# Norm guard and layernorm eps as pair reductions on VectorE, and the layer's input added one step sooner on GpSimd, in a two-block attention kernel

## Chip, cores and metric

The kernel runs on one core of a Trainium2 chip. The metric is the device time of one execution in microseconds; where several runs are given, their median stands with the lowest and the highest.

## The reference

The input is 16 sequences of 256 tokens with 128 channels, float32. Two blocks follow each other, each closed by a layernorm without gain over `x + block(x)`.

The first block is a gated depthwise convolution and a 16-head attention in which the keys are softmaxed in chunks of 64. The change does not touch it.

The second block has two layers. Cut to what matters, one of them is:

```python
h = shift_token(x); q, k, v = split(h @ wqkv)          # 8 heads of 64
q = q / clip(norm(q), 1e-12) * qs;  k = k / clip(norm(k), 1e-12) * ksc
q, k = rotary_xpos(q, k)
x = x + local_attention(q, k, v) @ wo                  # windows of 64, each sees itself and the one before
h = shift_token(x); h = (h - mean(h)) / sqrt(var(h) + 1e-5) * lg + lb
a, g = split(h @ w1 + b1)
x = x + (a * gelu(g)) @ w2 + b2
```

After the second layer the block's input is added once more and the last layernorm is taken.

## The kernel before, in words

Every engine has an instruction list of its own, written out by hand, with semaphores between them. Stage A computes the first block. Then the two layers run as one pipeline over 32 units, a unit being one sequence of one layer: 16 units of layer 0, then 16 of layer 1. A unit has two steps, one for each half of its tokens (`tile` 0, the even step, and `tile` 1, the odd step). In its steps each engine does work of several units, at lags that `F_LATE` sets in steps: the layernorm statistics of a unit come 4 steps after its scores, the GELU gates 6, the product of gates and values and the down projection 7, its residual sum `yo` 8, the final normalisation `zo` 9. A loop body holds four steps, that is two units.

In each step of the layers:

- TensorE computes the scores (L1427, L1434), transposes the normalised weights of the step before (L1448) as soon as GpSimd has normalised them (`f_normed`), makes the output projection (L1473), the projections of the next unit (L1360), the transposes of its q and k (L1365, after `qk_normed`), the weighted values (L1462) and pieces of the MLP (L1378, and the down projection L1399 at the end of the odd step, after VectorE's `uT`).
- VectorE takes the score maximum (`fmx`, L1191) and subtracts it (L1195). In odd steps the low part of the next input (L1141), the first product `uT` and the normalised middle `hc` (L1091) follow; in even steps `yo` (L1122), in layer 1 with the statistics of `yo`. Then `rotate` (L1072, L1073 and the reduction L1076 of the squares), `mid` (L1156), the sum of the exponentials (L1173) and its reciprocal (L1177). In odd steps the last two products `uT` (L1099) come next, in even steps the statistics of the middle (L1082, L1086). A second `rotate` ends the step, and in odd steps of layer 1 `zo` (L1134).
- GpSimd does for each of the two `rotate`s: the sum of the two rotated products (L649), the maximum of the squared norm with a floor (L657), the power -0.5 (L660) and the multiplication by it (L663). Between the two it normalises five of the eight heads' weights (L710) and, in even steps, takes the middle's rstd in two instructions, the eps addition (L684) and the power (L686). In layer 1 it adds the layer input at the end of an odd step (`residual`, L694), and begins odd steps with the rstd of `yo`, again L684 and L686.
- ScalarE squares the projections (L801), copies from PSUM, takes the exponentials (L893), scales three heads (L870) and computes the GELU (L848), each with a table load where the function changes. In layer 0 it keeps a copy of `mid` (`kept`, L863) where layer 1 has the residual; it reads the same entry of `F_LATE`.
- SyncE issues the DMAs in an order of its own: for each unit the loads of `hn` and `res`, the shifts of `mid` into `mn` (32 KB pieces), in layer 1 the load of `res1`, which the residual adds, and the stores.

What waits for what around the change:

- GpSimd's power waits for `guarded`, which today its own maximum sets; the maximum waits for `norm_step` of VectorE's reduction.
- VectorE's `mid` of a unit waits until the residual of the unit two before it is made (`resb_set` in layer 1, `mid_kept` in layer 0), since it writes the same buffer.
- The residual waits for both halves of `mid` of its unit, for `yo` of the unit two before it (`f_read["down"]`, the buffer `resb`) and for its DMA (`res1_in`).
- `hc` waits for `m_rstd`, `zo` for `z_rstd`.

Of the kernel before, what the change touches and what calls it, by code (L numbers as in the profile page):

```python
# [25 lines left out]
P = 128  # L26
# [12 lines left out]
PAIR = 2  # L39
# [8 lines left out]
F_LATE = {"stats": 4, "norm": 5, "residual": 5, "mT": 6, "gates": 6, "mix": 6, "values": 7, "down": 7, "yo": 8, "z": 9}  # L48
# [123 lines left out]
def build(nc, t):  # L172

    ctx = ExitStack()
    with ctx:
# [82 lines left out]
        norm2 = sb("norm2", [P, 2, 4 * F_HEADS])  # L258
# [29 lines left out]
        mmv = [sb(f"mmv{p}", [P, TILES, 2]) for p in range(PAIR)]  # L288
        mrstd = [sb(f"mrstd{p}", [P, 2, TILES]) for p in range(PAIR)]
        zstat = [sb(f"zstat{p}", [P, TILES, 6]) for p in range(PAIR)]  # L290
        zmv = [sb(f"zmv{p}", [P, TILES, 2]) for p in range(PAIR)]
# [45 lines left out]
        N_CONSTS, N_F_CONSTS, N_PADS = 7, 6, 4  # L337
# [254 lines left out]
        def _(pool):  # L592
            pool.memset(ones[:, :], 1.0).then_inc(consts_set, 1)
            pool.memset(halves[:, :], -0.5).then_inc(consts_set, 1)
            pool.memset(eps[:, :], LN_EPS).then_inc(consts_set, 1)
            for p in range(PAIR):
                pool.memset(uT[p][:, F_CHUNKS - 1, :], 1.0).then_inc(consts_set, 1)
# [46 lines left out]
            def layers_program():  # L644
# [7 lines left out]
                def normalise(unit, m):  # L652

                    at, index = slice(F_HEADS * m, F_HEADS * (m + 1)), 4 * unit + m
                    pool.wait_ge(consts_set, N_CONSTS)
                    pool.wait_ge(norm_step, index + 1)
                    nc.gpsimd.tensor_scalar_max(norm2[:, 1, at], norm2[:, 0, at], NORM_FLOOR).then_inc(guarded, 1)  # L657
                    pool.wait_ge(guarded, index + 1)
                    wait(pool, qk_normed, index - 3)
                    nc.gpsimd.tensor_tensor(out=rnorm[:, at], in0=norm2[:, 1, at], in1=halves[:, 0:F_HEADS], op=ALU.pow).then_inc(rnorm_set, 1)  # L660
# [20 lines left out]
                def rstd_of(mv2, out, step, done, stats, count):  # L681

                    pool.wait_ge(stats, TILES * (count + 1))
                    nc.gpsimd.tensor_tensor(out=out[:, 0, :], in0=mv2[:, :, 1], in1=eps[:, 0:TILES], op=ALU.add).then_inc(step, 1)  # L684
# [12 lines left out]
                def body(it, turn, layer_of):  # L697
                    for s, p, tile in f_steps(turn):
                        n, unit = F_STEPS * it + s, PAIR * it + p
                        local = f_late(turn, s, "z")  # L700
                        if local is not None and layer_of(local) == LAYERS - 1:
                            rstd_of(zmv[local % PAIR], zrstd[local % PAIR], z_eps, z_rstd, z_stats, PAIR * it + local - BATCH * (LAYERS - 1))
# [10 lines left out]
                        if local is not None:  # L713
                            rstd_of(mmv[local % PAIR], mrstd[local % PAIR], m_eps, m_rstd, m_stats, PAIR * it + local)
# [206 lines left out]
        def _(dve):  # L921
# [137 lines left out]
            def layers_program():  # L1059
                def rotate(index, before, local, m, turn, layer):  # L1060
# [15 lines left out]
                    nc.vector.tensor_reduce(norm2[:, 0, F_HEADS * m:F_HEADS * (m + 1)],  # L1076
                                            sq[m % 2][:, :].rearrange("p (h d) -> p h d", h=F_HEADS), AX.X, ALU.add).then_inc(norm_step, 1)

                def stats(x, st, out, bn, done, count):
# [5 lines left out]
                    for tile in range(TILES):  # L1085
                        nc.vector.bn_aggr(out[:, tile, :], st[:, tile, :]).then_inc(done, 1)  # L1086
# [490 lines left out]
```

## Time and profile before

| | us |
|---|---|
| median of 3 runs | 1403.01 (1402.93 to 1405.08) |
| the profiled execution | 1405.44 |
| its span | 1403.6 |
| VectorE busy | 1231.8 (88%) |
| GpSimd busy | 943.0 (67%) |
| TensorE matmul busy | 1249.5 (89%) |
| ScalarE busy | 944.8 (67%) |

The busy times come from the profiled execution, whose own time stands in the second line; what lies outside its span is 1.8 us. Shares are means over two stages with different limits: up to about 690 us the first block runs, after it the two layers. Instructions of one engine overlap at their ends in the records, so a next one may start some hundredths before the last one's end.

### The profile page before, as it was taken

Reading aid. Unit: us, or ns where it says so; the run is one execution under the profiler, and the core shown is the slowest. Engines: PE = TensorE matmul, PEld = TensorE weight load, DVE = VectorE, ACT = ScalarE, POOL = GpSimd, SP = SyncE. Lnnn points to the kernel's source line nnn. Section 1 sums busy time; section 2 is a strip of 40 time slices with the busy share of each in tenths; the row PEclk is TensorE's granted clock in tenths of the full one; section 3 lists DMA queues with packets and bytes.
Section 4 is the critical chain, followed back from the end, with each engine's and each line's share of the span. In section 5 each row is a group of like instructions: output and inputs, shape, how many; then the busy total and the mean of one; then the engine's idle time right before and its main releaser. Section 6 shows DMA issues by size and latency. Waiting matters only on the chain.

```text
span 1403.6 us, 36296 instructions
## 1 busy us (share of the span) xinstructions
PE 1249.5 (89%) x12288; PEld 977.4 (70%) x12288; DVE 1231.8 (88%) x2418; ACT 944.8 (67%) x1708; POOL 943.0 (67%) x915
## 2 busy tenths in 40 slices
PE   4799889898988988988788999999999999999986
PEld 3577667776767766766566777777777777677764
DVE  4899999999999999998488888988888888888873
ACT  3566565666665656664367888888888877778772
POOL 0734443444344334444799999999999999999971
PEclk9899999999999999998999999999999999999998
DMA  5000000000000000000111212111122122211110
GB/s 170 1 10 13 9 7 12 12 11 9 11 11 4 9 11 11 8 7 14 25 41 36 51 43 47 45 45 43 46 53 49 42 52 48 50 46 44 47 35 27
DMA packets 87052, 44.15 MB, mean 31 GB/s; under 512 B 43908, under 2 KB 80176, under 8 KB 86960
## 3 DMA queue, kind: packets, MB, share of 16 engines
q1 hardware_dynamic: 86960, 42.95, 12.3%
q8 instruction: 54, 0.88, 0.3%
q14 instruction: 38, 0.31, 0.1%
HBM read 19.86 MB, written 6.29 MB: 19 GB/s over the span
## 4 chain that ended last, share of the span: by engine, by line
DVE 36%; POOL 25%; issue 17%; PE 17%; SPq 2%; ACT 1%; DVEq 1%; POOLq 0%; DMA 0%; ACTq 0%
DVE sums L993 9%; POOL rnorm L660 9%; POOL kT L649 7%; DVE probs L1025 7%; DVE mx L1019 5%; POOL probs L710 3%; POOL kT L663 3%; PE bank L1399 2%; DVE xo L1054 2%; PE bank L1378 2%; PE bank L1360 2%; PE bank L1434 2%; SPq L476 1%; DVE conv L936 1%; PE bank L1462 1%
## 5 line engine op out<-in xcount | busy, mean ns | idle before, releaser
L625 POOL TENSOR_TENSOR probs<-probs,coef 128x1024 f32<-128x1024 f32 x128 | 239.6, 1903 | 201.2 <-DVE coef L985 201.2
L660 POOL TENSOR_TENSOR rnorm<-norm,halves 128x8 f32<-128x8 f32 x128 | 213.8, 1671 | 10.7
L785 ACT ACTIVATE probs<-probs 128x1024 f32<-128x1024 f32 x128 | 134.7, 1052 | 101.7 <-DVE probs L1025 101.2
L1280 PE MATMUL bank<-ident,probs 128*128 128x128 f32 x1024 | 143.1, 284 | 50.0 <-POOL probs L625 49.9
L772 ACT ACTIVATE wT<-bank 128x512 f32<-128x512 f32 x256 | 138.8, 596 | 63.6 <-PE bank L1280 62.4
L1019 DVE TENSOR_REDUCE mx<-bank 128x8 f32<-128x512 f32 x256 | 163.7, 680 | 14.7 <-PE bank L1293 13.3
L649 POOL TENSOR_TENSOR kT<-qT 128x512 f32<-128x512 f32 x128 | 163.8, 1280 | 8.4 <-DVE qT L1073 8.4
L1280 PEld LDWEIGHTS bank<-ident,probs 128*128 128x128 f32 x1024 | 115.4, 144 | 69.5 <-POOL probs L625 58.5
L1025 DVE TENSOR_TENSOR probs<-bank,mx 128x512 f32<-128x512 f32 x256 | 163.4, 679 | 0.0
L1293 PE MATMUL bank<-kT,qT 64*128 64x256 f32 x1024 | 154.7, 423 | 6.3 <-DVE probs L1025 6.3
L1319 PE MATMUL bank<-wT,v 128*64 128x128 f32 x2048 | 144.3, 284 | 11.0 <-DVE gate L931 6.2
L993 DVE TENSOR_REDUCE sums<-probs 128x16 f32<-128x1024 f32 x128 | 153.0, 1207 | 0.0
L1319 PEld LDWEIGHTS bank<-wT,v 128*64 128x64 f32 x2048 | 113.0, 140 | 49.6 <-issue 23.5
L663 POOL TENSOR_TENSOR kT<-kT,rnorm 128x512 f32<-128x512 f32 x128 | 133.7, 1044 | 10.0
L1191 DVE TENSOR_REDUCE fmx<-bank 128x4 f32<-128x512 f32 x128 | 82.3, 685 | 60.4 <-PE bank L1434 60.4
L1293 PEld LDWEIGHTS bank<-kT,qT 64*128 64x128 f32 x1024 | 93.3, 196 | 36.8 <-issue 23.3
L636 POOL TENSOR_TENSOR rstd<-mv,eps 128x1 f32<-128x1 f32 x32 | 6.2, 194 | 155.2 <-DVE mv L1048 155.2
L1378 PE MATMUL bank<-hT,w 128*128 128x256 f32 (+1 forms) x384 | 96.8, 388 | 3.8 <-DVE uT L1099 2.3
L1360 PE MATMUL bank<-wqkv_high,fhT_high 128*128 128x512 f32 x192 | 93.1, 485 | 0.2
L1448 PE MATMUL bank<-ident,probs 128*128 128x128 f32 x512 | 69.0, 278 | 26.9 <-POOL probs L710 26.7
L1072 DVE TENSOR_TENSOR qT<-bank,table 128x512 f32<-128x512 f32 x128 | 87.0, 680 | 5.4 <-ACT qT L801 5.4
L1448 PEld LDWEIGHTS bank<-ident,probs 128*128 128x128 f32 x512 | 56.1, 141 | 47.6 <-POOL probs L710 38.2
(120 smaller groups left out, 3082.7 us busy)
## 6 DMA issues: line engine op xcount, KB each, us to landing
probs<-f_v SPq DMA_DIRECT2D x96, 128.0 KB, 2.3
res<-stage_x SPq DMA_DIRECT2D x48, 128.0 KB, 3.9
xn<-in_x SPq DMA_DIRECT2D x16, 128.0 KB, 2.2
xr<-in_x SPq DMA_DIRECT2D x16, 128.0 KB, 2.2
stage_x<-xo SPq DMA_DIRECT2D x32, 64.0 KB, 1.6
hn<-stage_x SPq DMA_DIRECT2D x32, 64.0 KB
mn<-mid SPq DMA_DIRECT2D x64, 32.0 KB
stage_x<-yo SPq DMA_DIRECT2D x16, 128.0 KB, 2.1
```

The lines of the kernel that those rows point to most:

```text
L625: nc.gpsimd.tensor_tensor(out=e[:, :, :, :], in0=e[:, :, :, :], in1=coef[r][:, 2, A_REP * ng:A_REP * (ng + 1), :].unsqueeze(3).broadcast_t ...
L649: nc.gpsimd.tensor_tensor(out=qk[m][:, :, :], in0=on_self[m % 2][:, :, :], in1=on_partner[m % 2][:, :, :], op=ALU.add).then_inc(added, 1)
L660: nc.gpsimd.tensor_tensor(out=rnorm[:, at], in0=norm2[:, 1, at], in1=halves[:, 0:F_HEADS], op=ALU.pow).then_inc(rnorm_set, 1)
L663: nc.gpsimd.tensor_tensor(out=qk[m][:, :, :], in0=qk[m][:, :, :], in1=rnorm[:, at].unsqueeze(2).broadcast_to([P, F_HEADS, F_HD]), op=ALU.m ...
L772: nc.scalar.activation(wT[hp][:, :, :, :], banks[4 + hp][:, :], ACT.Copy).then_inc(wT_read, 1)
L785: nc.scalar.activation(e[:, :, :, :], e[:, :, :, :], ACT.Exp).then_inc(exp_done, 1)
L993: nc.vector.tensor_reduce(sums[at % 2][:, A_REP * gg:A_REP * (gg + 1), :], E[(s - SUM_LAG) % E_RING][:, :, :, :], AX.X, ALU.add).then_inc( ...
L1019: ins = nc.vector.tensor_reduce(m[:, 2 * k:2 * k + 2, :], both[k][:, :].rearrange("p (h c k) -> p h c k", h=2, c=CHUNKS), AX.X, ALU.max)
L1025: ins = nc.vector.tensor_tensor(e[:, 2 * k:2 * k + 2, :, :], both[k][:, :].rearrange("p (h c k) -> p h c k", h=2, c=CHUNKS), m[:, 2 * k:2 ...
L1280: ins = nc.tensor.transpose(banks[4 + hp][:, P * (2 * kb + hh):P * (2 * kb + hh + 1)], e[:, 2 * hh + hp, 2 * kb:2 * kb + 2, :], ident[:, :])
L1293: ins = nc.tensor.matmul(banks[2 * (s % 2) + h % 2][:, SEQ * (h // 2):SEQ * (h // 2 + 1)], qT[p][lo:lo + A_HD, 2 * g + h // 2, P * tile:P ...
L1319: ins = nc.tensor.matmul(bank[A_HD * hh:A_HD * (hh + 1), P * hp:P * (hp + 1)], v[ap][:, kb, A_HD * og:A_HD * (og + 1)], wT[hp][:, kb, hh, ...
```

## The change

The maximum with the norm floor and the eps additions of both layernorms in the layers leave GpSimd. Each becomes a reduction on VectorE over pairs, whose second member is a constant that a memset writes once: (squared norm, floor) under max, (variance, eps) under add. For that `norm2` holds pairs, the result goes to a buffer of its own, `norm2_held`, and the mean and variance buffers get a third column. VectorE's `held` comes in odd-numbered projections right behind `rotate`, in even-numbered ones behind `mid`. `stats` ends with a wait for its own aggregates and the eps reduction. GpSimd's residual, and with it ScalarE's copy in layer 0, is moved by `F_LATE` from 5 steps after the scores to 4, from the end of an odd step to the end of the even step ahead of it.

```diff
-F_LATE = {"stats": 4, "norm": 5, "residual": 5, "mT": 6, ...}
+F_LATE = {"stats": 4, "norm": 5, "residual": 4, "mT": 6, ...}
...
-        norm2 = sb("norm2", [P, 2, 4 * F_HEADS])
+        norm2 = sb("norm2", [P, 4 * F_HEADS, 2])
+        norm2_held = sb("norm2_held", [P, 4 * F_HEADS])
...
-        mmv = [sb(f"mmv{p}", [P, TILES, 2]) for p in range(PAIR)]
+        mmv = [sb(f"mmv{p}", [P, TILES, 3]) for p in range(PAIR)]
...
-        zmv = [sb(f"zmv{p}", [P, TILES, 2]) for p in range(PAIR)]
+        zmv = [sb(f"zmv{p}", [P, TILES, 3]) for p in range(PAIR)]
...
+            pool.memset(norm2[:, :, 1], NORM_FLOOR).then_inc(consts_set, 1)
+            for p in range(PAIR):
+                pool.memset(mmv[p][:, :, 2], LN_EPS).then_inc(consts_set, 1)
+                pool.memset(zmv[p][:, :, 2], LN_EPS).then_inc(consts_set, 1)
...
                 def normalise(unit, m):
-                    pool.wait_ge(consts_set, N_CONSTS)
-                    pool.wait_ge(norm_step, index + 1)
-                    nc.gpsimd.tensor_scalar_max(norm2[:, 1, at], norm2[:, 0, at], NORM_FLOOR).then_inc(guarded, 1)
                     pool.wait_ge(guarded, index + 1)
                     wait(pool, qk_normed, index - 3)
-                    nc.gpsimd.tensor_tensor(out=rnorm[:, at], in0=norm2[:, 1, at], in1=halves[:, 0:F_HEADS], op=ALU.pow).then_inc(rnorm_set, 1)
+                    nc.gpsimd.tensor_tensor(out=rnorm[:, at], in0=norm2_held[:, at], in1=halves[:, 0:F_HEADS], op=ALU.pow).then_inc(rnorm_set, 1)
...
-                def rstd_of(mv2, out, step, done, stats, count):
-                    pool.wait_ge(stats, TILES * (count + 1))
-                    nc.gpsimd.tensor_tensor(out=out[:, 0, :], in0=mv2[:, :, 1], in1=eps[:, 0:TILES], op=ALU.add).then_inc(step, 1)
+                def rstd_of(out, step, done, count):
                     pool.wait_ge(step, count + 1)
...
+                def held(index, before, m):
+                    at = slice(F_HEADS * m, F_HEADS * (m + 1))
+                    dve.wait_ge(norm_step, index + 1)
+                    wait(dve, rnorm_set, 4 * before + m + 1)
+                    nc.vector.tensor_reduce(norm2_held[:, at], norm2[:, at, :], AX.X, ALU.max).then_inc(guarded, 1)
...
                     for tile in range(TILES):
-                        nc.vector.bn_aggr(out[:, tile, :], st[:, tile, :]).then_inc(done, 1)
+                        nc.vector.bn_aggr(out[:, tile, 0:2], st[:, tile, :]).then_inc(done, 1)
+                    dve.wait_ge(done, TILES * (count + 1))
+                    nc.vector.tensor_reduce(rstd[:, 0, :], out[:, :, 1:3], AX.X, ALU.add).then_inc(step, 1)
...
                             rotate(4 * (unit + 1) + at, unit, 4 * (p + 1) + at, at, turn, layer_of(p + 1))
                         if f_exists(turn, s, F_XO_LAG):
                             attended(it, s, layer_of)
+                        if prepares(turn, p):
+                            held(4 * (unit + 1) + 2 * tile, unit, 2 * tile)
...
                             at = 2 * tile + 1
                             rotate(4 * (unit + 1) + at, unit, 4 * (p + 1) + at, at, turn, layer_of(p + 1))
+                            held(4 * (unit + 1) + at, unit, at)
```

## Rows read from the trace of the kernel before

**Rows 1.** Busy time of each engine in two units of layer 0.

```profile
core 0: us, PE busy (x) PEld busy (x) DVE busy (x) ACT busy (x) POOL busy (x), PEclk, DMA share, GB/s
...
841.30:882.60 41.30, 40.59 (x454) 32.31 (x453) 36.39 (x75) 34.51 (x65) 39.85 (x41) 1.00 0.19 45
```

**Rows 2.** Waits, whole run: total us, times, longest.

```profile
PEld bank L1448 <- POOL probs L710: 38.2, 42, 2.0
```

**Rows 3.** Timeline of GpSimd in layer 0: start us, duration us, then the instruction.

```profile
964.34 1.28 POOL L649 TENSOR_TENSOR kT<-qT 128x512 f32<-128x512 f32 x1
965.59 0.24 POOL L657 TENSOR_SCALAR norm<-norm 128x8 f32<-128x8 f32 x1
965.92 1.67 POOL L660 TENSOR_TENSOR rnorm<-norm,halves 128x8 f32<-128x8 f32 x1
...
969.88 0.20 POOL L684 TENSOR_TENSOR mrstd<-mmv,eps 128x2 f32<-128x2 f32 x1
970.15 0.70 POOL L686 TENSOR_TENSOR mrstd<-mrstd,halves 128x2 f32<-128x2 f32 x1
...
972.39 1.67 POOL L660 TENSOR_TENSOR rnorm<-norm,halves 128x8 f32<-128x8 f32 x1
974.14 1.04 POOL L663 TENSOR_TENSOR kT<-kT,rnorm 128x512 f32<-128x512 f32 x1
```

**Rows 4.** Timeline of VectorE in layer 0, an even and an odd step.

```profile
959.42 1.29 DVE L1191 TENSOR_REDUCE fmx<-bank 128x4 f32<-128x512 f32 x2 [1.41 <-PE bank L1434]
...
962.75 0.68 DVE L1073 TENSOR_TENSOR qT<-bank,table 128x512 f32<-128x512 f32 x1
...
964.14 1.21 DVE L1173 TENSOR_REDUCE f_sum<-probs 128x8 f32<-128x1024 f32 x1
965.39 0.20 DVE L1177 RECIPROCAL f_rsum<-f_sum 128x8 f32<-128x8 f32 x1
...
969.06 1.29 DVE L1191 TENSOR_REDUCE fmx<-bank 128x4 f32<-128x512 f32 x2 [0.87 <-PE bank L1434]
...
972.19 0.59 DVE L1091 TENSOR_SCALAR hc<-mn,mmv,mrstd 128x128 f32<-128x128 f32 x2
...
980.10 1.29 DVE L1191 TENSOR_REDUCE fmx<-bank 128x4 f32<-128x512 f32 x2 [1.41 <-PE bank L1434]
```

**Rows 5.** Timeline of TensorE, the down projection of that odd step.

```profile
976.96 1.60 PE L1399 MATMUL bank<-w,uT 128*128 128x128 f32 x12 [0.34 <-DVE uT L1099]
```

**Rows 6.** Timeline of VectorE and GpSimd in layer 1, an even step.

```profile
1170.54 1.29 DVE L1191 TENSOR_REDUCE fmx<-bank 128x4 f32<-128x512 f32 x2 [0.90 <-PE bank L1434]
...
1176.72 0.73 POOL L694 TENSOR_TENSOR resb<-mid,res 128x256 f32<-128x256 f32 x1
...
1177.48 0.29 DVE L1156 TENSOR_TENSOR mid<-bank,res 128x128 f32<-128x128 f32 x1 [1.32 <-POOL resb L694]
...
1181.66 1.28 DVE L1191 TENSOR_REDUCE fmx<-bank 128x4 f32<-128x512 f32 x2
```

**Rows 7.** Groups by line: the smallest reduction on VectorE (busy us, mean ns).

```profile
L952 DVE TENSOR_REDUCE gate_sum<-gate 128x1 f32<-128x3 f32 x16 | 2.5, 156 | 0.6
```

**Rows 8.** DMA issues: size each, median us from issue to landing.

```profile
res<-stage_x SPq DMA_DIRECT2D x48, 128.0 KB, 3.9
```

**Rows 9.** Timeline, start of the layers: a GpSimd sum that waited for VectorE.

```profile
696.81 0.68 DVE L1073 TENSOR_TENSOR qT<-bank,table 128x512 f32<-128x512 f32 x1
...
697.57 1.27 POOL L649 TENSOR_TENSOR kT<-qT 128x512 f32<-128x512 f32 x1 [6.85 <-DVE qT L1073]
```

**Rows 10.** Timeline, first hc of the run and GpSimd beside it.

```profile
743.48 1.28 POOL L649 TENSOR_TENSOR kT<-qT 128x512 f32<-128x512 f32 x1
743.54 1.29 DVE L1091 TENSOR_SCALAR hc<-mn,mmv,mrstd 128x128 f32<-128x128 f32 x1 [0.51 <-POOL mrstd L686]
744.76 0.34 DVE L1091 TENSOR_SCALAR hc<-mn,mmv,mrstd 128x128 f32<-128x128 f32 x1
```

**Rows 11.** Timeline of VectorE: first and last score maximum of the counted units.

```profile
762.43 1.29 DVE L1191 TENSOR_REDUCE fmx<-bank 128x4 f32<-128x512 f32 x2 [2.26 <-PE bank L1434]
...
1337.70 1.28 DVE L1191 TENSOR_REDUCE fmx<-bank 128x4 f32<-128x512 f32 x2
```

More of the change, by code:

```diff
@@ L46 @@
 F_ATT_LAG, F_XO_LAG = 1, 2
-F_LATE = {"stats": 4, "norm": 5, "residual": 5, "mT": 6, "gates": 6, "mix": 6, "values": 7, "down": 7, "yo": 8, "z": 9}
+F_LATE = {"stats": 4, "norm": 5, "residual": 4, "mT": 6, "gates": 6, "mix": 6, "values": 7, "down": 7, "yo": 8, "z": 9}
 F_KEYS = 2 * WINDOW
@@ L336, in build @@
         N_GATE_WEIGHTS, N_A_WEIGHTS, N_WEIGHTS = 5, 4, 2 + LAYERS * (6 + 3 * F_CHUNKS + 6)
-        N_CONSTS, N_F_CONSTS, N_PADS = 7, 6, 4
+        N_CONSTS, N_F_CONSTS, N_PADS = 12, 6, 4
         GATE_STEPS = 3
@@ L701, in body @@
                         if local is not None and layer_of(local) == LAYERS - 1:
-                            rstd_of(zmv[local % PAIR], zrstd[local % PAIR], z_eps, z_rstd, z_stats, PAIR * it + local - BATCH * (LAYERS - 1))
+                            rstd_of(zrstd[local % PAIR], z_eps, z_rstd, PAIR * it + local - BATCH * (LAYERS - 1))
                         if prepares(turn, p):
@@ L713, in body @@
                         if local is not None:
-                            rstd_of(mmv[local % PAIR], mrstd[local % PAIR], m_eps, m_rstd, m_stats, PAIR * it + local)
+                            rstd_of(mrstd[local % PAIR], m_eps, m_rstd, PAIR * it + local)
                         if prepares(turn, p):
@@ L1075, in rotate, with stats @@
                     wait(dve, guarded, 4 * before + m + 1)
-                    nc.vector.tensor_reduce(norm2[:, 0, F_HEADS * m:F_HEADS * (m + 1)],
+                    nc.vector.tensor_reduce(norm2[:, F_HEADS * m:F_HEADS * (m + 1), 0],
                                             sq[m % 2][:, :].rearrange("p (h d) -> p h d", h=F_HEADS), AX.X, ALU.add).then_inc(norm_step, 1)
-                def stats(x, st, out, bn, done, count):
+                def held(index, before, m):
[3 more added lines that the diff above has]
+                    nc.vector.tensor_reduce(norm2_held[:, at], norm2[:, at, :], AX.X, ALU.max).then_inc(guarded, 1)
+                def stats(x, st, out, rstd, bn, done, step, count):
                     for tile in range(TILES):
@@ L1125, in finished @@
                         dve.wait_ge(f_read["down"], unit + 1)
-                        stats(yo[par], zstat[par], zmv[par], z_bn, z_stats, b)
+                        stats(yo[par], zstat[par], zmv[par], zrstd[par], z_bn, z_stats, z_eps, b)
                 def closed(it, local):
@@ L1166, in beside @@
                             rotate(m, -1, m, m, "pre", 0)
+                            held(m, -1, m)
                     a_body(TURNS, "drain", beside)
@@ L1217, in body @@
                             dve.wait_ge(mn_in[par], 80 * (it + local // PAIR + 1))
-                            stats(mn[par], mstat[par], mmv[par], m_bn, m_stats, PAIR * it + local)
+                            stats(mn[par], mstat[par], mmv[par], mrstd[par], m_bn, m_stats, m_eps, PAIR * it + local)
                         if prepares(turn, p):
```

## The prediction, made before the changed kernel ran

> **What bounds the kernel now.** I read the page's 40 slices first: in the second half, the two layers, GpSimd is at nine tenths or more in nearly every slice. The busy time by stretch says so for two units of layer 0: GpSimd is busy 39.85 of 41.30 us, and TensorE 40.59 [rows 1]. So two engines are full at once, and the order of time must say which sets the pace. The list of waits for the whole run shows TensorE's weight loads waiting 38.2 us for GpSimd's normalised weights [rows 2]. GpSimd's timeline of one unit has each instruction behind the other with no bracket of idle time [rows 3]. VectorE's timeline has a gap of 1.41 us ahead of an even step's score maximum, ended by TensorE [rows 4]. In TensorE's timeline the down projection of an odd step is kept by VectorE's product, 0.34 us [rows 5].
>
> A unit is two steps. The odd step of layer 0 (start of the score maximum at 969.06, the next at 980.10) takes 11.04 us. It is a chain without GpSimd: VectorE from the maximum to the last uT, then TensorE's down projection and scores. The even step (959.42 to 969.06) takes 9.64 us, and TensorE is packed in it; over the stretch it was most often 9.62. Together 20.68 [rows 4]. GpSimd's own work is 20.65 a unit. So **in layer 0 two limits lie within 0.03 us of each other**, and whatever GpSimd gives back the VectorE and TensorE loop does not. Layer 1 is another case. GpSimd has the residual of 0.73 us and a second rstd more, and VectorE stands 1.32 us before `mid`, waiting for the residual [rows 6].
>
> **Part by part.** *GpSimd loses* the maximum: 965.59 to 965.92 in time, 0.33 us, four times a unit, 1.31; and the eps addition, 969.88 to 970.15, 0.27, once a unit in layer 0 and twice in layer 1 [rows 3]. Its work falls to 19.06 a unit in layer 0. Its wait list gains VectorE's `guarded`, with the exponentiation and everything behind it queued there. That wait is covered: the sum of 1.28 us runs first, and the held value is there about 0.8 us after it starts.
>
> *VectorE gains* four reductions of 16 to 8 columns a unit and one or two of 4 to 2. The trace has none of these. From below, the reduction of three columns takes 156 ns [rows 7]; from above, the reciprocal of 8 columns takes 0.20 us [rows 4]. A following instruction starts some 0.08 before the end of the one ahead (the second hc 0.25 after a first of 0.34 [rows 4, 10]), so I take 0.10 each. Where it must wait for the reduction just ahead, the lost overlap and 0.04 of latency (f_sum to reciprocal, 1.21 us and a start 1.25 later [rows 4]) make it 0.22. That is the second one of each step and those of the eps.
>
> - Odd step of layer 0: only the first held reduction lies before uT, +0.10. The second falls into the 1.41 us gap [rows 4].
> - Even step of layer 0: 0.10, 0.22 and 0.22 for the eps, 0.54 in all, into the gap of 0.87 ahead of the next maximum [rows 4]. Nothing. If that gap were gone all of it would count.
> - Layer 1, even step: 11.12 us now, with the 1.32 us wait [rows 6]. VectorE is full in the rest, so all it gets counts: 9.80 + 0.54, and about 0.1 for the second eps, make 10.4. Gain 0.7.
> - Layer 1, odd step: +0.10 before uT; the zo pair at its end comes 0.3 later. The gap at 1170.54 is 0.90 [rows 6].
>
> *The residual* moves from the end of an odd GpSimd step to the end of the even one before it. Its input from HBM is issued on SyncE's queue in the step before, behind `mid`, and nothing moves in that queue; it lands 3.9 us after its issue [rows 8], and GpSimd asks for it half a unit later. The other input frees with yo in the same even step, at its 2.4th us, ahead of GpSimd's turn. So the 1.32 us wait goes. ScalarE's copy in layer 0 moves too, since both read the same number. It then stands ahead of the GELU table load of the even step, 0.4 us, where ScalarE's next reader has more slack than that. Nothing. The five memsets at the start lie under the first loads. Nothing.
>
> **Where GpSimd lands next.** This decides. Once GpSimd is ahead it waits each step for VectorE's rotated product, so its phase is fixed to VectorE's. In the even step the product ends at 962.75 + 0.68, which is 4.01 after the maximum's start, and GpSimd starts 0.08 after such an end (697.57 against 696.81 + 0.68 [rows 9]): 4.09. From that sum to the second multiplication of the step it takes 974.14 - 964.34 = 9.80, less two maxima and one eps: 8.87 [rows 3]. Sum 12.96, less an even step of 9.62: the multiplication starts at 3.34 of the odd step. Now hc: a pair of TENSOR_SCALARs on VectorE that starts at 3.13 of the odd step, the second 0.25 later at 3.38 [rows 4, 10]. At 743.54 the trace has such a hc under a GpSimd sum that had started 0.06 before it: it took 1.29 instead of 0.34 us, to 0.07 after the sum's end. Its twin at 744.76 was not held [rows 10]. At 972.19, with hc beside the exponentiation, nothing was lost [rows 3, 4]. So at present hc falls just ahead of the exponentiation; afterwards its second half meets a multiplication of 1.04 us that began 0.04 before it. It would end at 3.34 + 1.04 + 0.07 = 4.45 instead of 3.72: **+0.73 on the chain that sets the odd step**.
>
> [...]
>
> **The sum.**
> - Layer 0: 0.73 + 0.10 - 0.02 (TensorE no longer waits for GpSimd in the even step) = +0.81 a unit. From 762.43 to 1337.70 [rows 11] are 27 units, 16 of them of layer 0's kind; one or two at its ends miss the meeting. 15 x 0.81 = +12.2.
> - Layer 1: the 11 units that follow. Even step -0.7. Odd step: counting on GpSimd's pieces from its multiplication at 3.7, its normalising of the weights starts at 10.1 and takes 1.26, and the second zo ends behind it at 11.4; less the overlap of 0.08 the next maximum starts at 11.3 instead of 11.1, +0.25. Together -0.45 in the nine units that have the whole pattern: -4.1.
> - The first seven steps of the layers, before 762.43: TensorE there waits for GpSimd's weights, and each of six steps is shortened by the two maxima, 0.66: -3.9. The bound is [rows 2], 38.2 us over the run.
> - Ends and drain: -0.5.
>
> Sum +3.7. The profiled execution took 1405.44 us (span 1403.6); the median of the three runs is 2.43 below it. I put the change on the median: 1403.01 + 3.7 = 1406.7, so +0.26%. About 0.2% (2.8 us) is what a measurement of this kernel can tell from no change.
>
> **Rivals.**
> 1. *The meeting doesn't happen, and it gets faster* (0.30). Deciding place: the second hc against the multiplication, a margin of 0.04 us from my sum. If the multiplication starts over about 0.1 later than I say, hc goes first. Then layer 0 pays 0.08 a unit (+1.3), and layer 1, the start and the drain give -8.5 or so less what the zo meeting eats: 1403.01 - 8.5 = 1394.5. For it: today's phase of hc, which the trace shows harmless in 16 units. Against it: in today's kernel GpSimd's phase is set by its own fullness, and that is what goes.
> 2. *Layer 1 meets too* (0.14). There zo starts at about 9.9 of the odd step and the weights' normalising at 10.1. If the reductions cost 0.03 more than 0.10 each, the even step grows by four of them, and zo's first half also falls behind the weights, its second behind the next sum: it ends at 12.5, +1.2 a unit in 11 units. 1406.7 + 13 = 1420.
> 3. *Only some units meet* (0.10): the margins are smaller than the jitter. Between 1395 and 1405, say 1400.
> 4. *The reductions cost far more than the rows near them* (0.06), 0.25 each with the waits: the even step of layer 0 fills its 0.87 gap and rival 2 comes in addition. 1412 and more.
> 5. *Nothing moves, since TensorE binds at 20.6*: true of layer 0 alone. Layer 1's 1.32 us wait is VectorE's, so as a whole I give it no chance of its own; it lies in the forecast's lower edge.
>
> **How the numbers follow.** The forecast has 0.40, with its own range 1403.5 to 1410 (the reductions between 0.08 and 0.14 each, one to three units without the meeting). Faster by over 0.2%: rival 1 and half of rival 3, 0.35. Within 0.2%: the other half of rival 3 and the lowest quarter to third of the forecast, 0.17. Slower: the rest, 0.48. The range takes in rival 1 with its bounds down to 1391 and rival 2's middle at 1420.
>
> **What would show it.** hc of odd steps with a second half of about 1.07 us in layer 0, directly behind a GpSimd multiplication; layer 0's unit at 21.5 instead of 20.68; GpSimd idle some 2 us a unit before its sums, ended by VectorE; no wait of `mid` for resb; layer 1's even step near 10.4. The forecast is wrong if hc stays at 0.59 a pair (rival 1), or if the wait before `mid` stays.

## The result, and the profile after the change

The changed kernel takes 1395.89 us, the median of 5 runs (1392.71 to 1396.14). The kernel before took 1402.95 (1402.14 to 1405.08) beside it. The ratio is 0.9942 [0.9927, 0.9956]: **0.6% faster**, 7.1 us, where 1406.7 was forecast and a gain had the chance 0.35. The profiled execution took 1395.98 us.

The page: span, busy times, and the chain that ended last. Then two of its groups.

```profile
span 1394.2 us, 36286 instructions
...
PE 1245.1 (89%) x12288; PEld 982.3 (70%) x12288; DVE 1268.7 (91%) x2594; ACT 938.3 (67%) x1708; POOL 901.6 (65%) x744
...
DVE 50%; issue 23%; PE 15%; POOL 8%; SPq 2%; DVEq 1%; ACT 1%; DMA 0%; POOLq 0%; ACTq 0%
...
L654 POOL TENSOR_TENSOR kT<-qT 128x512 f32<-128x512 f32 x128 | 163.5, 1277 | 52.3 <-DVE qT L1073 39.0
...
L1201 DVE TENSOR_REDUCE fmx<-bank 128x4 f32<-128x512 f32 x128 | 82.3, 685 | 34.8 <-PE bank L1447 34.7
```

The roles have changed. GpSimd is busy 41.4 us less than before and now stands before its sums, mostly for VectorE's rotated product. VectorE is busy 36.9 us more and carries half of the chain (GpSimd 8%; before it was 36% and 25%). TensorE's weight loads, which stood 38.2 us for GpSimd's weights [rows 2], stand 10.5 us for them. From the list of waits of the layers (us in total, times, longest):

```profile
ACT hT L855 <- PE bank L1396: 86.3, 32, 6.2
POOL kT L654 <- DVE qT L1073: 38.7, 35, 6.9
DVE fmx L1201 <- PE bank L1447: 34.7, 40, 3.8
...
PEld bank L1461 <- POOL probs L710: 10.5, 13, 1.7
```

Two lines, the new reductions in the view of one source line (duration ns least, median, most; first and last start):

```profile
L1084 DVE TENSOR_REDUCE norm_held<-norm x128: 148/169/172, 666.3 to 1340.5; 128x8 f32<-128x16 f32 x128
...
L1095 DVE TENSOR_REDUCE mrstd<-mmv x32: 156/157/159, 733.0 to 1374.0; 128x2 f32<-128x4 f32 x32
```

**Where the time went** comes out of the score maxima of VectorE, which mark the steps. These are the 1st, 8th, 40th, 62nd and 64th of the changed kernel in VectorE's timeline:

```profile
691.56 0.69 DVE L1201 TENSOR_REDUCE fmx<-bank 128x4 f32<-128x512 f32 x1 [3.81 <-PE bank L1447]
...
755.70 1.29 DVE L1201 TENSOR_REDUCE fmx<-bank 128x4 f32<-128x512 f32 x2 [1.57 <-PE bank L1447]
...
1090.21 1.29 DVE L1201 TENSOR_REDUCE fmx<-bank 128x4 f32<-128x512 f32 x2 [0.32 <-PE bank L1447]
...
1331.14 1.28 DVE L1201 TENSOR_REDUCE fmx<-bank 128x4 f32<-128x512 f32 x2
...
1350.52 1.29 DVE L1201 TENSOR_REDUCE fmx<-bank 128x4 f32<-128x512 f32 x2 [1.47 <-PE bank L1447]
```

The same five marks in each profile cut the span into parts (us). "Layer 0" is steps 7 to 39, sixteen odd steps; "layer 1" is steps 39 to 61, eleven units. The labels are those of the experiments below.

| kernel | start of layers | first seven steps | layer 0 | layer 1 | last two steps | rest | span |
|---|---|---|---|---|---|---|---|
| before | 693.81 | 68.62 | 331.12 | 244.15 | 21.34 | 44.6 | 1403.6 |
| changed | 691.56 | 64.14 | 334.51 | 240.93 | 19.38 | 43.7 | 1394.2 |
| changed again (11) | 691.18 | 64.18 | 334.48 | 240.33 | 19.40 | 43.6 | 1393.2 |
| hc first (1) | 691.61 | 64.16 | 330.68 | 239.92 | 19.40 | 47.1 | 1392.9 |
| hc later (2) | 691.69 | 64.19 | 339.45 | 240.83 | 19.40 | 44.7 | 1400.3 |
| eps back (3) | 691.66 | 64.42 | 331.00 | 242.08 | 20.18 | 43.1 | 1392.4 |
| residual back (4) | 691.45 | 64.16 | 336.04 | 246.39 | 19.96 | 41.9 | 1399.9 |
| hc first, zo early (5) | 690.94 | 64.16 | 330.66 | 237.58 | 19.36 | 48.1 | 1390.8 |
| residual alone (6) | 691.24 | 68.58 | 331.17 | 244.03 | 22.35 | 44.2 | 1401.6 |
| guard alone (7) | 689.61 | 64.50 | 330.93 | 235.28 | 19.51 | 44.1 | 1383.9 |
| guard, hc first, zo early (8) | 690.53 | 64.61 | 331.01 | 232.21 | 20.17 | 46.7 | 1385.2 |
| guard, zo early (9) | 691.86 | 64.39 | 330.94 | 232.22 | 19.47 | 44.5 | 1383.4 |
| eps alone (10) | 693.78 | 68.36 | 329.34 | 239.16 | 20.84 | 45.5 | 1397.0 |

From before to changed: first steps -4.5, layer 0 +3.4, layer 1 -3.2, last two steps -2.0, the rest -0.9, together -7.2; the medians differ by 7.1. The profiled spans differ by 9.4. The 2.3 left are the start of the layers, which moves between 689.6 and 693.8 from profile to profile, the kernels without the guard edit among them (691.24 and 693.78), so that these profiles don't show whether any of it is the change's.

**Layer 0, the meeting.** An odd step of the changed kernel in VectorE's and then in GpSimd's timeline:

```profile
1028.58 0.47 DVE L1108 SCALAR_TENSOR_TENSOR uT<-bank,b,ge 85x256 f32<-85x256 f32 x1
1028.97 1.35 DVE L1100 TENSOR_SCALAR hc<-mn,mmv,mrstd 128x128 f32<-128x128 f32 x2
1030.24 0.68 DVE L1072 TENSOR_TENSOR qT<-bank,table 128x512 f32<-128x512 f32 x1
...
1026.24 1.28 POOL L654 TENSOR_TENSOR kT<-qT 128x512 f32<-128x512 f32 x1
1027.47 1.65 POOL L662 TENSOR_TENSOR rnorm<-norm_held,halves 128x8 f32<-128x8 f32 x1
1029.20 1.04 POOL L665 TENSOR_TENSOR kT<-kT,rnorm 128x512 f32<-128x512 f32 x1
```

And the same place three units earlier:

```profile
966.57 0.47 DVE L1108 SCALAR_TENSOR_TENSOR uT<-bank,b,ge 85x256 f32<-85x256 f32 x1
966.96 0.59 DVE L1100 TENSOR_SCALAR hc<-mn,mmv,mrstd 128x128 f32<-128x128 f32 x2
...
964.32 1.28 POOL L654 TENSOR_TENSOR kT<-qT 128x512 f32<-128x512 f32 x1
965.57 1.65 POOL L662 TENSOR_TENSOR rnorm<-norm_held,halves 128x8 f32<-128x8 f32 x1
967.29 1.16 POOL L665 TENSOR_TENSOR kT<-kT,rnorm 128x512 f32<-128x512 f32 x1
```

The second `hc` starts 0.25 after the first. In the first of the two units the multiplication starts 0.23 after the first `hc`, and the pair takes 1.35 instead of 0.59: the second `hc` is held, that is, it ends only behind the multiplication, the forecast meeting. In the second it starts 0.33 after it; nothing happens to `hc`, and the multiplication is the one that takes longer, 1.16 instead of 1.04. A unit of the first kind has an odd step of 11.91 us, one of the second 11.11 to 11.15. **Of the sixteen units five are held**, and a sixth just behind step 39. In both of these cases the instruction whose start came first, by 0.02 and by 0.08, kept its usual time (the multiplication 1.04, the `hc` pair 0.59), and the other one took longer. That was not so beside GpSimd's power, and in experiment 3, where starts lay 0.01 to 0.06 apart, the order in the records did not decide (both in the last section).

**Layer 1.** VectorE's maximum and `zo` at the end of an odd step, GpSimd beside it:

```profile
1200.17 1.29 DVE L1201 TENSOR_REDUCE fmx<-bank 128x4 f32<-128x512 f32 x2
...
1209.99 1.58 DVE L1143 TENSOR_SCALAR zo<-yo,zmv,zrstd 128x128 f32<-128x128 f32 x2
1211.49 1.28 DVE L1201 TENSOR_REDUCE fmx<-bank 128x4 f32<-128x512 f32 x2
...
1210.23 1.26 POOL L710 TENSOR_TENSOR probs<-probs,f_rsum 128x640 f32<-128x640 f32 x1
1211.45 1.28 POOL L654 TENSOR_TENSOR kT<-qT 128x512 f32<-128x512 f32 x1
```

`zo` begins 0.24 before GpSimd's normalising of the weights, its second half starts 0.05 after it and is held to its end (1.29 instead of 0.34). The even step of layer 1 is 10.5 us (before, 11.12 [rows 6] and 11.25 in turn), the odd one 11.32 and 11.43 in turn (11.03 and 11.17), and `mid` no longer waits for the residual. VectorE's maximum has no bracket here: VectorE is full in both steps.

### The profile page after: what moved, and what is told of

Its sections match the earlier page's. It is cut to its first block, busy times and chain, and to the rows that moved or that the text cites. A ratio compares the mean times of both kernels' runs of the same rounds, so it can differ in the third digit from the quotient of the medians.

```text
span 1394.2 us, 36286 instructions
## 1 busy us (share of the span) xinstructions
PE 1245.1 (89%) x12288; PEld 982.3 (70%) x12288; DVE 1268.7 (91%) x2594; ACT 938.3 (67%) x1708; POOL 901.6 (65%) x744
## 3 DMA queue, kind: packets, MB, share of 16 engines
q1 hardware_dynamic: 86960, 42.95, 12.1%
## 4 chain that ended last, share of the span: by engine, by line
DVE 50%; issue 23%; PE 15%; POOL 8%; SPq 2%; DVEq 1%; ACT 1%; DMA 0%; POOLq 0%; ACTq 0%
DVE sums L993 9%; DVE probs L1025 7%; DVE mx L1019 4%; POOL kT L654 3%; DVE f_sum L1183 3%; DVE qT L1073 3%; PE bank L1412 2%; DVE norm L1076 2%; DVE xo L1054 2%; PE bank L1447 2%; PE bank L1373 2%; DVE qT L1072 2%; PE bank L1391 1%; DVE probs L1205 1%; SPq L477 1%
## 5 line engine op out<-in xcount | busy, mean ns | idle before, releaser
L662 POOL TENSOR_TENSOR rnorm<-norm_held,halves 128x8 f32<-128x8 f32 x128 | 211.6, 1653 | 0.0
L1293 PE MATMUL bank<-ident,probs 128*128 128x128 f32 x1024 | 142.5, 284 | 49.4 <-POOL probs L630 49.4
L1293 PEld LDWEIGHTS bank<-ident,probs 128*128 128x128 f32 x1024 | 114.9, 144 | 68.6 <-POOL probs L630 57.9
L1332 PE MATMUL bank<-wT,v 128*64 128x128 f32 x2048 | 144.1, 284 | 11.3 <-DVE gate L931 5.7
L1072 DVE TENSOR_TENSOR qT<-bank,table 128x512 f32<-128x512 f32 x128 | 87.4, 683 | 4.3 <-ACT qT L801 3.5
L801 ACT ACTIVATE qT<-bank 128x512 f32<-128x512 f32 x128 | 75.8, 592 | 18.2 <-PE bank L1373 10.7
L1073 DVE TENSOR_TENSOR qT<-bank,table 128x512 f32<-128x512 f32 x128 | 87.0, 680 | 0.0
```

The costliest lines, as they stand in the source:

```text
L662: nc.gpsimd.tensor_tensor(out=rnorm[:, at], in0=norm2_held[:, at], in1=halves[:, 0:F_HEADS], op=ALU.pow).then_inc(rnorm_set, 1)
L1293: ins = nc.tensor.transpose(banks[4 + hp][:, P * (2 * kb + hh):P * (2 * kb + hh + 1)], e[:, 2 * hh + hp, 2 * kb:2 * kb + 2, :], ident[:, :])
L1332: ins = nc.tensor.matmul(bank[A_HD * hh:A_HD * (hh + 1), P * hp:P * (hp + 1)], v[ap][:, kb, A_HD * og:A_HD * (og + 1)], wT[hp][:, kb, hh, ...
```

## The experiments

Theory: the forecast's meeting is right, with its price, and only the count of units that meet is off; so what moves `hc` out of the way or further in moves layer 0 by 0.8 us a unit. Rival: the long odd steps have another cause. For the gains: which of the three edits brings them, and is one of them a loss? Five of the expectations name the theory after a port. No trace here shows one: what the runs show is which instruction is held, for how long, and where the other one stood (second `hc` 1.10 us instead of 0.34, with the multiplication 0.23 after the first). "Before" below is the kernel before, run beside each.

**1. hc first.** `hc` put ahead of the first `uT`.

```diff
+                        if late("norm") is not None:
+                            normalised(late("norm") % PAIR, PAIR * it + late("norm"))
                         if late("values") is not None:
                             mixed(it, late("values"), layer_of(late("values")))
-                        if late("norm") is not None:
-                            normalised(late("norm") % PAIR, PAIR * it + late("norm"))
```

> The changed kernel with hc (the two TENSOR_SCALARs of the normalised middle) ahead of the first uT instead of behind it; same instructions, hc starts 0.40 us earlier in the odd step (2.7 instead of 3.1). Port theory: in the changed kernel the second hc takes 1.10 instead of 0.34 us in 6 of 16 units of layer 0, where GpSimd's multiplication starts 0.23 after the first hc, and 0.34 where it starts 0.33 after. Moved 0.4 earlier, both halves lie under the exponentiation: no hc over 0.4 us, every unit of layer 0 at 20.65, 6 x 0.80 = 4.8 us less than the changed kernel, about 1391. Rival (the loop is longer by VectorE's added reductions and nothing else): the order of hc and uT plays no part, 1395.9.

Measured: 1394.3 us (1392.3 to 1394.7), 0.993 [0.991, 0.995]. All odd steps of layer 0 are 11.10 to 11.16, and layer 0 is 3.8 us shorter: the meeting is what made the long ones. The whole gained less than that, since the rest is 3.4 longer. There (the drain, the last 47 us) `hc` stands 1.6 us for its rstd with `uT` queued behind it, and `mid` stands 2.2 us for TensorE instead of 0.7:

```profile
DVE mid L1165 <- PE bank L1486: 2.2, 2, 1.9
DVE hc L1100 <- POOL mrstd L686: 1.6, 2, 0.8
```

So in the drain `hc` is late, and the new order makes `uT` wait behind it. That this is the whole 3.4 us was not tested. The other two kernels with this order have 48.1 and 46.7 as well.

**2. hc later.** One small reduction more, of constants into an unused buffer, between the first `uT` and `hc`.

```diff
+                            nc.vector.tensor_reduce(spare[:, :], ones[:, 0:16].rearrange("p (a b) -> p a b", b=2), AX.X, ALU.max)
```

> The changed kernel with one more small reduction (8 columns from 16, about 0.09 us) ahead of hc in each odd step, so that hc starts 0.09 later and the multiplication lies at 0.14 to 0.24 behind the first hc. It writes a buffer that nothing reads. Port theory: the second hc at 1.1 to 1.2 us in all 16 units of layer 0, the odd step at 12.0, 10 more units at 0.8 and 16 at 0.09: about 9 us more than the changed kernel, 1405. Rival (added work only): 27 x 0.09 = 2.4 us more, 1398.

Measured: 1400.65 (1397.62 to 1404.08), 0.9975 [0.9961, 0.9989]; layer 0 is 4.9 longer than in the changed kernel, with ten held odd steps (11.95) of sixteen, and an eleventh behind step 39. The direction is right, "all sixteen" is not. This run showed why. A held unit, VectorE and GpSimd:

```profile
1030.83 1.29 DVE L1202 TENSOR_REDUCE fmx<-bank 128x4 f32<-128x512 f32 x2 [0.32 <-PE bank L1449]
...
1033.96 0.15 DVE L1213 TENSOR_REDUCE spare<-ones 128x8 f32<-128x16 f32 x1
1034.03 1.31 DVE L1101 TENSOR_SCALAR hc<-mn,mmv,mrstd 128x128 f32<-128x128 f32 x2
...
1031.24 1.29 POOL L655 TENSOR_TENSOR kT<-qT 128x512 f32<-128x512 f32 x1
...
1034.21 1.06 POOL L666 TENSOR_TENSOR kT<-kT,rnorm 128x512 f32<-128x512 f32 x1
```

and a free one:

```profile
967.14 1.29 DVE L1202 TENSOR_REDUCE fmx<-bank 128x4 f32<-128x512 f32 x2 [0.26 <-PE bank L1449]
...
970.34 0.59 DVE L1101 TENSOR_SCALAR hc<-mn,mmv,mrstd 128x128 f32<-128x128 f32 x2
...
967.62 1.29 POOL L655 TENSOR_TENSOR kT<-qT 128x512 f32<-128x512 f32 x1
968.87 1.85 POOL L663 TENSOR_TENSOR rnorm<-norm_held,halves 128x8 f32<-128x8 f32 x1
970.80 1.05 POOL L666 TENSOR_TENSOR kT<-kT,rnorm 128x512 f32<-128x512 f32 x1
```

Count from the maximum. GpSimd's sum starts at 0.41 in the one and 0.48 in the other. There are two groups of units in every kernel with the guard on VectorE: seven (odd steps 9, 11 and 29 to 37) in which GpSimd is early, and eight (13 to 27) in which it is 0.08 later, because the sum of the even step ahead starts 0.08 or 0.16 after the rotated product it waited for. (Step 7, the sixteenth, is a different case, with the multiplication 0.80 after `hc`, and never held.) In the changed kernel the multiplication would start at about 3.36 or 3.44 and the second `hc` stands at 3.38. Here the second `hc` stands 0.08 later, at 3.46. Held units of the two groups:

| | second hc less multiplication, early group | late group | held of 7 early | held of 8 late |
|---|---|---|---|---|
| changed | 0.00 to 0.03 | -0.07 to -0.05 | 5 | 0 |
| changed again (11) | -0.01 to 0.03 | -0.08 to -0.06 | 5 | 0 |
| residual back (4) | 0.02 to 0.04 | -0.07 to -0.04 | 7 | 0 |
| hc later (2) | 0.07 to 0.10 | 0.00 to 0.03 | 7 | 3 |

The distances are estimates from the rows of each unit: the second `hc` is the first plus 0.25, and the multiplication, as if nothing held it, is the start of the sum plus 2.96 (1.23 to the power and 1.73 from there). Where GpSimd is ahead by 0.04 or more all units are held, where it is behind by 0.04 or more none. Between 0.00 and 0.03 both happen. In the changed kernel the two free units of the early group are those with 0.00, and the five held ones have 0.02 or 0.03; but in run 11 units with 0.00 were held too, and here two with 0.03 went free. The rows have hundredths, and finer than that they don't tell.

**3. Eps back on GpSimd**, guard on VectorE and residual at 4.

```diff
-                    dve.wait_ge(done, TILES * (count + 1))
-                    nc.vector.tensor_reduce(rstd[:, 0, :], out[:, :, 1:3], AX.X, ALU.add).then_inc(step, 1)
...
+                    pool.wait_ge(stats, TILES * (count + 1))
+                    nc.gpsimd.tensor_tensor(out=out[:, 0, :], in0=mv2[:, :, 1], in1=eps[:, 0:TILES], op=ALU.add).then_inc(step, 1)
```

> The changed kernel with both eps additions back on GpSimd (the norm guard stays on VectorE, the residual at 4). GpSimd's second multiplication of the even step then starts 0.27 later, 0.50 behind the first hc. Port theory: no hc held, layer 0 at 20.65 a unit, -4.8. In layer 1 the even step loses 0.3 us of VectorE work (10.2), but zo (at 9.8 of the odd step) now meets a multiplication that starts at about 9.75 and then the weights behind it: zo pair 2.2 us, odd step 12.0, +0.2 a unit, +2.5. In all 1393 to 1394. Rival (GpSimd's and VectorE's amounts of work decide): layer 0 unchanged, layer 1 -0.3 x 11, 1392.5, with hc still held in some units.

Measured: 1393.06 (1390.48 to 1394.17), 0.9922 [0.9902, 0.9942]. Layer 0 has no held unit: the eps addition on GpSimd puts its multiplication at 3.6 to 3.7 of the odd step, behind `hc`. In layer 1 the even step is 10.0, the odd one 12.1, since `zo` now meets a multiplication with its first half and the weights with its second (VectorE, then GpSimd):

```profile
1206.54 2.36 DVE L1143 TENSOR_SCALAR zo<-yo,zmv,zrstd 128x128 f32<-128x128 f32 x2
...
1206.56 1.04 POOL L665 TENSOR_TENSOR kT<-kT,rnorm 128x512 f32<-128x512 f32 x1
1207.56 1.26 POOL L712 TENSOR_TENSOR probs<-probs,f_rsum 128x640 f32<-128x640 f32 x1
```

The expectation had both meetings and the 12.0. Here the multiplication starts 0.02 after `zo` in the records and holds it all the same.

**4. Residual back at 5**, the changed kernel otherwise (guard and eps on VectorE).

```diff
-F_LATE = {"stats": 4, "norm": 5, "residual": 4, ...}
+F_LATE = {"stats": 4, "norm": 5, "residual": 5, ...}
```

> The changed kernel with the residual (and ScalarE's copy) back at 5 steps, the rest as changed. Theory: GpSimd is no longer full, so the residual at the odd step's end is made at about 4.0 to 4.7 of the next even step and mid at 5.8 does not wait for it. But it no longer stands between the multiplication and the rstd of the odd step, GpSimd's weights come 0.6 earlier, ahead of zo, and zo is held by them and by the sum behind: zo pair over 2 us, odd step of layer 1 near 11.9, +0.5 a unit, about 1401. Rival (the move is what takes the wait away): mid waits for resb again, over 1 us a unit of layer 1, 1405 or more.

Measured: 1403.5 (1400.85 to 1404.44), 0.9993 [0.998, 1.0006]: no gain is left. Layer 1's odd step takes 11.86 to 11.97, and there is no wait of `mid`; here too both halves of `zo` are held (VectorE, then GpSimd):

```profile
1213.55 2.12 DVE L1143 TENSOR_SCALAR zo<-yo,zmv,zrstd 128x128 f32<-128x128 f32 x2
...
1213.09 1.26 POOL L710 TENSOR_TENSOR probs<-probs,f_rsum 128x640 f32<-128x640 f32 x1
1214.31 1.28 POOL L654 TENSOR_TENSOR kT<-qT 128x512 f32<-128x512 f32 x1
```

Without the residual ahead of it in the odd step, the normalising of the weights starts 0.46 before `zo`; in the changed kernel it starts 0.24 after it. The moved residual is worth 0.5% here (0.9942 against 0.9993), and in another way than by its wait: it sets where GpSimd stands when `zo` comes.

**5. hc first and zo early**, the changed kernel with `hc` as in 1 and `zo` between the last `uT` and the second rotation.

```diff
+                        if late("z") is not None and layer_of(late("z")) == LAYERS - 1:
+                            closed(it, late("z"))
...
-                        if late("z") is not None and layer_of(late("z")) == LAYERS - 1:
-                            closed(it, late("z"))
```

> hc ahead of the first uT, and in layer 1 zo moved from the end of the odd step to between the last uT and the second rotate, at about 7.8 of the odd step, under GpSimd's exponentiation (7.4 to 9.1) instead of under the weights' normalising. Port theory: the zo pair takes 0.59 instead of 1.6 to 1.7 us, the odd step of layer 1 falls from 11.35 to the 11.1 that TensorE needs, 11 x 0.2 = 2.3 us less than with hc first alone: 1392. Rival (VectorE's amount of work decides in layer 1): same instructions, no change, 1394.3.

Measured: 1391.04 (1388.46 to 1394.09), 0.9909 [0.9892, 0.9927]. The odd step of layer 1 is 11.11, `zo` 0.59 a pair. As expected, with the longer drain of experiment 1.

**6. Residual alone**: the kernel before with `F_LATE` at 4.

> The kernel before with the residual at 4 steps and nothing else. Theory: the wait of mid for resb goes, but GpSimd has the same work and no gap, so its 22.28 us a unit of layer 1 stay and VectorE waits elsewhere for the same time: within 2 us of the kernel before. The start of the layers (first score maximum at 693.8) stays as before, if the 2 us that the changed kernel is earlier there come from the norm guard. Rival (the residual's wait is a cost by itself): 11 x 1.3 = 14 us less.

Measured: 1402.75 (1400.98 to 1405.36), 0.9995 [0.9986, 1.0004]. The wait of `mid` is gone from the list, yet layer 1 is unchanged (244.03). Between 1100 and 1328, where `mid` stood 12.7 us for the residual before, VectorE now stands 23.7 us for TensorE ahead of its maximum, 10.4 before, so the wait has only moved. TensorE's matmuls and loads still stand 14.2 and 13.9 us for GpSimd's weights (14.7 and 16.7 before), and GpSimd has as much to do as before. The residual's wait, on which the forecast's view of layer 1 rests [rows 6], cost nothing while GpSimd set the pace.

**7. Guard alone**: the maximum on VectorE, eps on GpSimd, residual at 5 (the edits of 3 and 4 together).

> The kernel before with the norm guard on VectorE and nothing else: eps on GpSimd, residual at 5. Theory: the start of the layers 2 us earlier and the first seven steps 4 us shorter, as in the changed kernel; layer 0 at 20.65 in every unit, hc not held since the multiplication starts 0.27 later; in layer 1 GpSimd's odd step is short of the residual and the zo pair falls differently: even step 10.0, and an odd step between 11.1 (not held) and 12.0 (both held). 1389 to 1396. No wait of mid for resb. Rival (each of the three parts gives its share): a third to a half of the changed kernel's gain, 1399 to 1401.

Measured: 1386.05 (1385.49 to 1387.3), 0.9879 [0.9862, 0.9896], **nearly ten us less than the changed kernel**. Its `hc` in layer 0, and the multiplication 0.34 us behind the second half:

```profile
963.74 0.59 DVE L1100 TENSOR_SCALAR hc<-mn,mmv,mrstd 128x128 f32<-128x128 f32 x2
...
964.33 1.04 POOL L665 TENSOR_TENSOR kT<-kT,rnorm 128x512 f32<-128x512 f32 x1
```

Layer 0 costs what it cost before (330.93). In layer 1 the even step is 10.0 us, not 10.5, since the two eps reductions with their waits are not there, and the odd one 11.41 to 11.45.

**8. Guard, residual at 4, hc first and zo early.**

> The norm guard on VectorE and the residual at 4, eps left on GpSimd, hc ahead of the first uT, zo between the last uT and the second rotate. Port theory: no hc and no zo held; layer 0 at 20.65; layer 1 with an even step of 10.0 and an odd one of 11.1, against 10.5 and 11.35 in the changed kernel: 11 x 0.75 = 8 us less there and 4 in layer 0, about 1385 to 1387. Rival (zo still meets GpSimd's sum, which is to end within 0.3 us of zo's start there): odd step 12 or more, 1393.

Measured: 1387.34 (1387.01 to 1388.06), 0.9887 [0.9871, 0.9904]. Layer 1 has 10.0 and 11.11 and is 3.1 shorter than in 7, layer 0 is the same, and the drain gives 2.6 back.

**9. Guard and zo early**: kernel 7 with `zo` moved as in 5, but left at its old place in the drain. (`zo` is the final normalisation; the expectation calls it the key scaling by mistake.)

```diff
+                        if prepares(turn, p) and late("z") is not None and layer_of(late("z")) == LAYERS - 1:
+                            closed(it, late("z"))
...
-                        if late("z") is not None and layer_of(late("z")) == LAYERS - 1:
+                        if not prepares(turn, p) and late("z") is not None and layer_of(late("z")) == LAYERS - 1:
```

> The guard alone on VectorE (the operations of the guard alone, residual at its old step) with the key scaling zo put between the last uT and the second rotation of its block, except in the drain behind the last steps, where it stays at its old place. My theory: of a layer-1 unit only the odd step changes, from 11.4 to 11.1 us, because zo no longer meets the GpSimd addition (the pair of zo falls from 1.67 to about 0.6 to 1.0); 11 units by 0.3 are 3 us, layer 0 stays at 331, and with zo back at its old place in the drain the tail stays at 44 as with the guard alone: about 1383 against 1386. Rival: zo meets something else there or the drain is longer anyway, as with both moves together: 1387 or no gain over 1386.

Measured: 1384.67 (1383.33 to 1387.01) beside 1405.3 for before, 0.9851 [0.9835, 0.9867]: **the lowest median of all, 1.5% below before**. VectorE in the odd step of layer 1, then GpSimd's power beside `zo`:

```profile
1192.89 1.29 DVE L1201 TENSOR_REDUCE fmx<-bank 128x4 f32<-128x512 f32 x2
...
1200.71 0.60 DVE L1143 TENSOR_SCALAR zo<-yo,zmv,zrstd 128x128 f32<-128x128 f32 x2
...
1204.00 1.29 DVE L1201 TENSOR_REDUCE fmx<-bank 128x4 f32<-128x512 f32 x2 [0.69 <-PE bank L1449]
...
1200.31 1.64 POOL L662 TENSOR_TENSOR rnorm<-norm_held,halves 128x8 f32<-128x8 f32 x1
```

11.11 us instead of 11.42, and a gap before the maximum again. Layer 1 is 3.06 shorter than in 7, as expected, and the rest 44.5. Against 7 the gain is shown in layer 1; in the whole the two intervals just overlap.

**10. Eps alone** on VectorE, guard on GpSimd, residual at 5.

> The kernel before with the eps addition alone on VectorE, the guard left on GpSimd, residual at its old step. My theory: layer 0 keeps its 331 us, since there GpSimd is not what sets the step, unless hc is held in more units; in layer 1 GpSimd sets 22.2 us of a unit, and 0.54 us (the eps addition with its turn) off GpSimd in each gives 4 to 7 us over 11 units: 1396 to 1399. Rival: the eps reduction costs VectorE what GpSimd saves, or the freed time goes to another wait: 1401 to 1404.

Measured: 1398.69 (1395.55 to 1398.9), 0.9944 [0.993, 0.9958]. Layer 1 is 5.0 shorter, 0.45 of a unit; layer 0 1.8 shorter, its even steps at 9.53 instead of 9.62. GpSimd is still without a gap in layer 1.

**11. The changed kernel again.**

> The changed kernel once more, word for word, in a profile of its own. My theory: the number of units of layer 0 in which the second hc is held by the GpSimd multiplication is no property of the program (the wait of GpSimd's sum ends 0.08 or 0.16 us after its releaser), so that another count than 6 of 16 comes out, and the span of layer 0 between steps 7 and 39 differs from 334.5 by 0.8 us for each unit more or less; the time stays within 1392 to 1399. Rival: the same 6 units meet again, and layer 0 takes 334.5 us again: then the phase belongs to the program.

Measured: 1394.59 (1393.67 to 1398.17), 0.9925 [0.991, 0.9939]. Layer 0 took 334.48, with five held units again, though not the same: the odd step at 29 was held and that at 37 was not, and the one at 39 was not. Neither expectation was right as written. The group of seven was the same in both profiles; which of the seven meet was not.

**Taken together**, with the residual at 5:

| | guard on GpSimd | guard on VectorE |
|---|---|---|
| eps on GpSimd | 1 (before) | 0.9879 (7) |
| eps on VectorE | 0.9944 (10) | 0.9993 (4) |

Each move gains alone, and both together gain nothing. The changed kernel, with both and the residual at 4, has 0.9942. While GpSimd sets the pace of layer 1, 0.54 us off it in a unit is 0.45 us gained. Once the guard has gone, VectorE sets it, and the same edit adds 0.5 us to VectorE's even step, and brings GpSimd's multiplication under `hc` in layer 0 and its weights under `zo` in layer 1.

## Why the prediction was wrong, point by point

- **What bounds before**: right for layer 0. For layer 1 the reading was wrong: the wait of `mid` [rows 6] was real but not the bound. Removing it alone brought nothing (6), while work taken off GpSimd shortened layer 1 in 7 and 10. GpSimd's own length was the bound.
- **The new reductions**: right. They take 148 to 172 ns, and the instruction behind one of the norm starts 0.08 to 0.10 us after its start where it waits for nothing; the eps with its wait costs 0.24, forecast 0.22 (the next rotation starts at 3.98 of the even step in layer 1, in kernel 7 at 3.74). The forecast's sum has no meeting for them, and none shows in the changed kernel: all 128 of the norm and 41 of the 48 of the eps overlap a GpSimd instruction, and they took 148 to 172 ns and 156 to 160 ns.
- **The meeting and its price**: right. 3.34 was forecast for the multiplication, 3.35 measured in the early group, the even step's sum at 4.09 as forecast, and a held unit costs 11.91 - 11.13 = 0.78 us; 0.73 was forecast.
- **The step that failed is "15 x 0.81 = +12.2"**, and in it "GpSimd starts 0.08 after such an end", taken from one row [rows 9] for all units. In eight of sixteen units the release took 0.16, so that the multiplication fell 0.05 to 0.07 behind the second `hc`, where the sum had it 0.04 ahead. In the seven others the margin was 0.00 to 0.03, and two went free. Five units were held and not fifteen, and layer 0 grew by 3.4 us. Ten units at 0.81 are 8.1 of the 8.8 missing. The rest is the term -0.02 for the even step, which lost 0.08 (9.54 for 9.62). That is the case of rival 3, which stood at 0.10 because I took margins of hundredths as fixed.
- **Layer 1, -4.1**: -3.2 measured, and with the held unit behind step 39 taken out (0.8) -4.0. Its steps were 10.5 and 11.3 to 11.4 for 10.4 and 11.3. Rival 2 did not come in the changed kernel, but it did in 4, where GpSimd's weights come 0.7 us earlier, and in another form in 3, where they come 0.8 later and a multiplication holds the first half of `zo`.
- **First seven steps, -3.9**: -4.5, and it is the guard's (64.1 to 64.6 in all kernels with it on VectorE, 68.4 to 68.6 without).
- **Ends and drain, -0.5**: -2.8, of it -2.0 in the last two steps. It was not worked out. Most of it goes with the guard (19.4 to 20.2 against 20.8 to 22.4).
- The differences add up: 12.2 - 3.4 = 8.8 in layer 0, 0.6 and 2.3 in the start and the drain, less 0.9 in layer 1, make 10.8. From +3.7 that gives -7.1.
- **Rival 1's number has an error in its sum.** It counts 1.3 for layer 0 and -8.5 for the other parts and then gives 1403.01 - 8.5 = 1394.5; with the 1.3 it is 1395.8. That this is the measured time to 0.1 us is luck: rival 1 said that no unit meets, and five did. With all seven of the early group held, as in 4, layer 0 alone would have taken some 1.5 us more.

What puts a unit in the early or the late group stays open. The groups are the same in all kernels. The one before has them too: its odd steps of layer 0 take 11.08 in the early group and 11.03 or 11.04 in the late one. So they come with the program's course and not with this edit; I made no experiment on it.

## What to carry to other kernels

Take load off an engine only as long as it is the bound: after the first cut ask again which engine is, since the second cut may be paid by the new one, as the eps reductions were. An engine that is freed changes its phase to the others, so every place where two engines can hold each other (here a `tensor_scalar` pair beside GpSimd, 0.59 us free and 1.35 to 2.36 held in the rows above) must be gone through again, with the order of starts to some hundredths of a microsecond. Where such a margin is smaller than the spread of a release, forecast a share of units and not all or none, or move the instruction to where it meets nothing; and check the drain by itself, where the moves of `hc` and `zo` cost 2.6 to 4.4 us here (1, 5, 8).

## What was not expected of the hardware

- The hold showed both ways. In the changed kernel a multiplication that starts 0.02 or 0.03 us before the second `hc` holds it for 0.76 us (1.10 instead of 0.34). One that comes 0.08 after it takes 0.12 us longer itself (1.16 instead of 1.04), or, in experiment 2, is recorded later behind a longer power (1.85 instead of 1.65).
- Near a tie the order of the recorded starts did not decide. In experiment 3 the multiplication starts 0.02 us after `zo` and holds it (1206.56 and 1206.54), in other units there up to 0.06 after.
- No `zo` was held by GpSimd's power on 8 columns in experiment 9, although the power started first. There `zo` starts at 1200.71, under a power from 1200.31 to 1201.95, and takes 0.60 as usual; in all ten units of layer 1 between 1116 and 1307 it starts 0.38 to 0.42 after the power, and the pair takes 0.59 or 0.60. Held to the power's end, as `hc` was to the sum's end [rows 10], the one at 1200.71 would have ended at about 1202.0.
- The same wait of GpSimd for the same VectorE instruction ends 0.08 us after it in some units and 0.16 in others, in runs of neighbouring units: in layer 0 of the changed kernel the sums that waited start 0.16 after the product from 813.95 to 968.91, and 0.08 after it before and behind that.
